# Edge stage of a graph network: block sums in float32r in two parts, and gathered rows in a ring of six quads

## Reference

```python
msg_in = jnp.concatenate([x[src], x[dst], edge_attr], axis=-1)
msgs = jnp.maximum(msg_in @ mW1 + mb1, 0.0) @ mW2 + mb2
agg = jax.ops.segment_sum(msgs, dst, num_segments=num_nodes)
cnt = jax.ops.segment_sum(jnp.ones((dst.shape[0],), x.dtype), dst, num_segments=num_nodes)
...
msg = h[src] + h_edge_attr
agg = jax.ops.segment_sum(msg, dst, num_segments=n)
```

## Time and profile before

| | us |
|---|---|
| median of three timed runs | 4918.04 (4917.9 to 4919.48) |
| span of the profiled execution | 5506.7 |
| PE busy, PEld busy | 4490.6, 3990.8 |
| DVE busy | 3075.2 |
| ACT busy | 1937.4 |
| POOL busy | 2459.1 |
| mean granted TensorE clock | 0.916 of full |

### The profile page before, as it was taken

One profiled execution on the slowest core, in us unless ns is written; L12 is line 12 of the kernel. 1 busy time (PEld: TensorE's weight loads), 2 busy tenths in 40 slices (PEclk: granted clock), 3 DMA queues, 4 the chain that ended last, 5 costly groups with the idle time before them and its releaser, 6 DMA issues. The chain is left out here.

```text
span 5506.7 us, 112775 instructions
## 1 busy us (share of the span) xinstructions
PE 4490.6 (82%) x38465; PEld 3990.8 (72%) x38465; DVE 3075.2 (56%) x7918; ACT 1937.4 (35%) x4103; POOL 2459.1 (45%) x2823
## 2 busy tenths in 40 slices
PE   0499999999666777777777877787778999888887
PEld 0399999999555666666666766676667666788887
DVE  5699999998333333333333333333334444688788
ACT  0556666665211111111111111111112444555666
POOL 5411111110466566566666656666662100465565
PEclk9799999999777888888888888888889999999999
DMA  4344444444444555555555555555557555666665
GB/s 107 130 199 210 210 210 209 201 202 201 145 113 126 156 162 165 155 163 160 164 162 158 164 162 164 159 164 164 165 168 209 182 187 187 204 208 208 221 216 181
DMA packets 571498, 966.86 MB, mean 176 GB/s; under 512 B 101223, under 2 KB 418775, under 8 KB 552519
## 3 DMA queue, kind: packets, MB, share of 16 engines
q1 hardware_dynamic: 407520, 767.32, 39.7%
q0 software_dynamic: 60048, 125.37, 8.8%
q10 hardware_dynamic: 103767, 72.40, 5.3%
HBM read 707.25 MB, written 257.60 MB: 175 GB/s over the span
## 5 line engine op out<-in xcount | busy, mean ns | idle before, releaser
L1022 POOL DMA_INDIRECT BIG<-table,BIG x1715 | 1697.2, 990 | 1166.0 <-DVE BIG L2454 557.6
L2454 DVE TENSOR_TENSOR BIG<-ps,BIG 128x512 f32<-128x512 f32 (+1 forms) x441 | 297.2, 674 | 1308.1 <-issue 905.6
L1822 PE MATMUL ps<-BIG 128*128 128x257 f32 x3430 | 953.3, 421 | 75.8 <-issue 44.5
L1822 PEld LDWEIGHTS ps<-BIG 128*128 128x128 f32 x3430 | 691.8, 213 | 210.3 <-issue 81.7
L1262 ACT ACTIVATE BIG<-BIG 128x512 f32<-128x512 f32 (+1 forms) x441 | 273.5, 620 | 1583.5 <-DVE BIG L2454 1318.4
L1837 PE MATMUL ps<-H_R,EXACT 128*128 128x256 f32 x4802 | 634.4, 288 | 96.6 <-DVE EXACT L2642 65.2
L1552 PE MATMUL ps<-H,ACC 128*128 128x128 f32 x4802 | 689.9, 284 | 0.0
L1837 PEld LDWEIGHTS ps<-H_R,EXACT 128*128 128x128 f32 x4802 | 591.9, 192 | 120.9 <-DVE EXACT L2642 88.0
L1810 PE MATMUL ps<-ACC,BIG 128*128 (+1 forms) x5145 | 525.1, 236 | 149.0 <-issue 131.9
L1552 PEld LDWEIGHTS ps<-H,ACC 128*128 128x128 f32 x4802 | 588.0, 191 | 0.2 <-ACT ACC L1203 0.2
L1810 PEld LDWEIGHTS ps<-ACC,BIG 128*128 128x128 bf16 x5145 | 420.1, 106 | 223.2 <-issue 186.2
(11 more groups left out here) (293 smaller groups left out, 7915.4 us busy)
## 6 DMA issues: line engine op xcount, KB each, us to landing
weight_mat<-ACC SPq DMA_DIRECT2D x49, 3136.0 KB, 9.2
BIG<-in_edge_attr SPq DMA_DIRECT2D x392, 256.0 KB
X<-count_mat SPq DMA_DIRECT2D x98, 800.0 KB, 4.4
count_mat<-BIG SPq DMA_DIRECT2D x49, 1568.0 KB, 12.8
X<-count_mat SPq DMA_DIRECT2D x98, 768.0 KB, 4.3
REL_WT<-weight_mat SPq DMA_DIRECT2D x275, 256.0 KB
BIG<-rel_tab ACTq DMA_DIRECT2D x392, 128.0 KB
BIG<-weight_mat SPq DMA_DIRECT2D x176, 256.0 KB
```

Source lines behind the costliest of these rows:

```text
L1022: pool.indirect_dma_start(G[:, q * QUAD + u, :], None, tables[1], bass.IndirectOffsetOnAxis(ap=STEP_IDX[:, b % 3, r * QUAD + u:r * QUAD + ...
L1822: mm = pe.matmul(PS[4 + par][:, 0:2 * F + 1], D[q * QUAD + u], HE[:, q * QUAD + u, :], start=(r == 0 and u == 0), stop=(r == QB - 1 and u ...
L2454: dve.tensor_tensor(HE[:, steps, 0:F], PS[n % 2][:, 0:size * F].rearrange("p (u f) -> p u f", f=F), G[:, steps, :], ALU.add).then_inc(rows ...
```

## The change

ReLU rows and attributes are each written twice, as a float32r part and as what it leaves (HI and LO_R), and the f32 product of a step becomes two float32r products, 258 and 256 columns wide, into the same sums. The first part of the attributes is a Copy on ACT, its rest a subtraction on DVE; the first part of the ReLU rows is the ReLU itself, now written to HI, its rest max(row, 0) minus HI on DVE. The gathered rows land in GR, a ring of six quads, are summed in place, and a place is free when the rest of the ReLU rows is made (`hidden_lo`). The attributes land in ATTR, a ring of four quads. The one-hots are written as float32r. The sums of a block leave PSUM in two copies, and ACC's space holds the new rings. DVE's order at position n becomes: turned one-hots, one-hots and attributes' rest of n, sum of n-1, weight group sums, ReLU rows' rest of n-1, then the rest as before.

```diff
--- before.py
+++ after.py
...
 QB = len(SIZES)
 QN = BLOCKS * QB
 EQ = 3
-GATHERS = [sum(SIZES[m % QB] for m in range(n % EQ, n + 1, EQ)) for n in range(QN)]
+GQ = 6
+AQ = 4
+GATHERS = [sum(SIZES[m % QB] for m in range(n % GQ, n + 1, GQ)) for n in range(QN)]
 DONE = [(b + 1) * QB for b in range(BLOCKS)]
 BLOCK_DONE = {n: b for b, n in enumerate(DONE)}
...
+        def of_acc(at, n):
+            return ACCf[:, at:at + n], at + n
+
+        HI_AT, LO_AT, DR_AT = 0, EQ * QUAD * HIW, EQ * QUAD * (HIW + 2 * F)
+        HI = nc.alloc_sbuf_tensor_at("HI", [P, EQ * QUAD, HIW], FP32R, offset=big_at + HI_AT * 4)
+        LO_R = nc.alloc_sbuf_tensor_at("LO_R", [P, EQ * QUAD, 2 * F], FP32R, offset=big_at + LO_AT * 4)
+        DR = nc.alloc_sbuf_tensor_at("DR", [P, EQ * QUAD, P], FP32R, offset=big_at + DR_AT * 4)
+        DTB_, at = of_big(DR_AT + EQ * QUAD * P, EQ * QUAD * P // 2)
+        DTB = DTB_.bitcast(BF16).rearrange("p (s f) -> p s f", f=QUAD * P)
+        STEP_, at = of_big(at, 3 * BSTEPS)
+        STEP_IDX = STEP_.bitcast(I32).rearrange("p (k s) -> p k s", s=BSTEPS)
+        assert at <= 7 * 2 * FSRC * P
+        HIDDEN_T, at = of_big(7 * 2 * FSRC * P, P)
+        NEW_B, at = of_big(at, P)
+        assert at <= 9232
+        ATT_, at = of_acc(0, BLOCKS * (F + 1))
+        ATT = ATT_.rearrange("p (b f) -> p b f", f=F + 1)
+        HS_, at = of_acc(-(-at // 16) * 16, 3 * F)
+        HS = [HS_[:, k * F:(k + 1) * F] for k in range(3)]
+        QP_, at = of_acc(at, 2 * PARTS * F // 2)
+        QP = [QP_[:, k * PARTS * F // 2:(k + 1) * PARTS * F // 2].bitcast(BF16) for k in range(2)]
+        ATTR_, at = of_acc(at, AQ * QUAD * F)
+        ATTR = ATTR_.rearrange("p (s f) -> p s f", f=F)
+        GR_, at = of_acc(at, GQ * QUAD * F)
...
             def attr_part(n, first):
-                r, q = n % QB, n % EQ
-                if n >= EQ:
-                    sp.wait_ge(quad_summed, n - EQ + 1)
-                sp.dma_start(HE[:, q * QUAD:q * QUAD + SIZES[r], F:2 * F],
+                r, q = n % QB, n % AQ
+                if n >= AQ:
+                    sp.wait_ge(attr_lo, ATTR_LO0 + n - AQ + 1)
+                sp.dma_start(ATTR[:, q * QUAD:q * QUAD + SIZES[r], :],
                              attr128[bass.ds(first + r * QUAD * P, SIZES[r] * P), :].rearrange("(u p) f -> p u f", p=P)).then_inc(attr_in[q], 16)
 
...
 
             def edge_gathers():
                 for n in range(QN):
-                    b, r, q = n // QB, n % QB, n % EQ
+                    b, r, q = n // QB, n % QB, n % GQ
                     if r == 0:
                         pool.wait_ge(staged, b + 1)
-                    if n >= EQ:
-                        pool.wait_ge(rows_added, n - EQ + 1)
+                    if n >= GQ:
+                        pool.wait_ge(hidden_lo, HIDDEN_LO0 + n - GQ + 1)
                     for u in range(SIZES[r]):
-                        pool.indirect_dma_start(G[:, q * QUAD + u, :], None, tables[1],
-                                                bass.IndirectOffsetOnAxis(ap=STEP_IDX[:, b % 3, r * QUAD + u:r * QUAD + u + 1], axis=0)).then_inc(gathered[q], 16)
+                        pool.indirect_dma_start(GR[:, q * QUAD + u, :], None, tables[1],
+                                                bass.IndirectOffsetOnAxis(ap=STEP_IDX[:, b % 3, r * QUAD + u:r * QUAD + u + 1], axis=0)).then_inc(rows_in[q], 16)
 
             pool.sem_inc(acc_ready, 1)
...
 
+            def attr_rounded(n):
+                r, q, g = n % QB, n % EQ, n % AQ
+                act.wait_ge(attr_in[g], 16 * (n // AQ + 1))
+                if n >= EQ:
+                    act.wait_ge(quad_summed, n - EQ + 1)
+                act.activation(HI[:, q * QUAD:q * QUAD + SIZES[r], F:2 * F], ATTR[:, g * QUAD:g * QUAD + SIZES[r], :], ACT.Copy).then_inc(attr_hi, 1)
+
             def dense_quad(n):
-                r, q = n % QB, n % EQ
+                r, q, g = n % QB, n % EQ, n % GQ
                 act.wait_ge(rows_added, n + 1)
                 if r == 0 and 1 <= n // QB < BLOCKS - 2:
                     stage_block(n // QB + 2)
-                hidden = HE[:, q * QUAD:q * QUAD + SIZES[r], 0:F]
-                act.activation(hidden, hidden, ACT.Relu).then_inc(relu_done, 1)
+                act.activation(HI[:, q * QUAD:q * QUAD + SIZES[r], 0:F], GR[:, g * QUAD:g * QUAD + SIZES[r], :], ACT.Relu).then_inc(relu_done, 1)
                 if n + EQ < QN:
                     load_edges(n + EQ)
 
             def q_part1(b):
-                act.activation(ACCB[:, b, 0:F], T1[:, b, :], ACT.Copy).then_inc(q_high, 1)
+                act.activation(QP[b % 2][:, 0:F], T1[:, b, :], ACT.Copy).then_inc(q_high, 1)
 
             def q_part2(b):
                 act.wait_ge(q_rest, PASSED + b + 1)
-                act.activation(ACCB[:, b, F:2 * F], T1[:, b, :], ACT.Copy).then_inc(q_mid, 1)
+                act.activation(QP[b % 2][:, F:2 * F], T1[:, b, :], ACT.Copy).then_inc(q_mid, 1)
 
             def act_quad(i, q, more):
...
@@ -1421,7 +1458,10 @@
                 act.wait_ge(q_sb, C1 + 1)
                 q_part1(0)
                 q_part2(0)
+                attr_rounded(0)
                 for n in range(POSITIONS):
+                    if n + 1 < QN:
+                        attr_rounded(n + 1)
                     if n < QN:
                         dense_quad(n)
                     if n in PARTS_AT:
...
                     for k in range(PARTS):
-                        pe.matmul(to, DTB[:, q, u * P:(u + 1) * P], ACCB[:, b, k * F:(k + 1) * F], start=(k == 0), stop=False)
+                        pe.matmul(to, DTB[:, q, u * P:(u + 1) * P], QP[par][:, k * F:(k + 1) * F], start=(k == 0), stop=False)
                     mm = pe.matmul(to, A18[:, q, u * P:(u + 1) * P], w18[:, :], start=False, stop=True)
                 mm.then_inc(pre_ps, 1)
 
             def dense_sums(b, r, par):
                 q = r % EQ
-                pe.wait_ge(relu_done, b * QB + (r + 1))
                 pe.wait_ge(onehot_ready, b * QB + (r + 1))
-                pe.wait_ge(attr_in[q], b * (16 * QB // EQ) + 16 * (r // EQ + 1))
+                pe.wait_ge(attr_lo, b * QB + (r + 1 + ATTR_LO0))
+                pe.wait_ge(hidden_lo, b * QB + (r + 1 + HIDDEN_LO0))
                 if r == 0 and (not isinstance(b, int) or b >= 2):
                     pe.wait_ge(block_out, b + (PASSED - 1))
                 for u in range(SIZES[r]):
-                    mm = pe.matmul(PS[4 + par][:, 0:2 * F + 1], D[q * QUAD + u], HE[:, q * QUAD + u, :],
-                                   start=(r == 0 and u == 0), stop=(r == QB - 1 and u == SIZES[r] - 1))
+                    one = DR[:, q * QUAD + u, :]
+                    pe.matmul(PS[4 + par][:, 0:HIW], one, HI[:, q * QUAD + u, :], start=(r == 0 and u == 0), stop=False)
+                    mm = pe.matmul(PS[4 + par][:, 0:2 * F], one, LO_R[:, q * QUAD + u, :], start=False, stop=(r == QB - 1 and u == SIZES[r] - 1))
                 mm.then_inc(quad_summed, 1)
 
...
-                dve.wait_ge(gathered[q], GATHERED0 + 16 * GATHERS[n])
+                r, g = n % QB, n % GQ
+                steps, size = slice(g * QUAD, g * QUAD + SIZES[r]), SIZES[r]
+                dve.wait_ge(rows_in[g], ROWS0[g] + 16 * GATHERS[n])
                 dve.wait_ge(pre_ps, n + 1)
+                dve.tensor_tensor(GR[:, steps, :], PS[n % 2][:, 0:size * F].rearrange("p (u f) -> p u f", f=F), GR[:, steps, :], ALU.add).then_inc(rows_added, 1)
+
+            def dense_attr_rest(n):
+                r, q, g = n % QB, n % EQ, n % AQ
+                steps, own = slice(q * QUAD, q * QUAD + SIZES[r]), slice(g * QUAD, g * QUAD + SIZES[r])
+                dve.wait_ge(attr_hi, ATTR_HI0 + n + 1)
                 if n >= EQ:
                     dve.wait_ge(quad_summed, n - EQ + 1)
-                dve.tensor_tensor(HE[:, steps, 0:F], PS[n % 2][:, 0:size * F].rearrange("p (u f) -> p u f", f=F), G[:, steps, :], ALU.add).then_inc(rows_added, 1)
+                dve.tensor_tensor(LO_R[:, steps, F:2 * F], ATTR[:, own, :], HI[:, steps, F:2 * F], ALU.subtract).then_inc(attr_lo, 1)
+
+            def dense_hidden_rest(n):
+                r, q, g = n % QB, n % EQ, n % GQ
+                steps, own = slice(q * QUAD, q * QUAD + SIZES[r]), slice(g * QUAD, g * QUAD + SIZES[r])
+                dve.wait_ge(relu_done, n + 1)
+                dve.scalar_tensor_tensor(LO_R[:, steps, 0:F], GR[:, own, :], 0.0, HI[:, steps, 0:F], ALU.max, ALU.subtract).then_inc(hidden_lo, 1)
 
             def dense_onehots(n):
                 r, q = n % QB, n % EQ
                 if n >= EQ:
                     dve.wait_ge(quad_summed, n - EQ + 1)
                 step, size = n // QB * BSTEPS + r * QUAD, SIZES[r]
-                dve.tensor_tensor(D_[:, q * QUAD * P:(q * QUAD + size) * P].rearrange("p (u d) -> p u d", d=P),
+                dve.tensor_tensor(DR[:, q * QUAD:q * QUAD + size, :],
                                   iota[:, :].rearrange("p (a d) -> p a d", a=1).broadcast_to([P, size, P]),
```

(21 more changed lines are left out.)

34 lines of the change are left out of this document (17 added, 17 removed).

## The result

The changed kernel takes 5010.8 us (median of four runs, 5007.5 to 5012.4) against 4918.0 us before: a ratio of 1.0191, 95% interval 1.0178 to 1.0203. That is 93 us more; the forecast was 182 us more. The sign and the kind of cause hold (gathers on POOL held up by operations on DVE), the size of that term does not.

What follows compares the result with a forecast made beforehand. The prediction took POOL's gathers to bound the edge stage in timed runs. It added 180 us for gathers delayed by DVE and 0 for all else to 4918, giving 5098, said as 5100 us, range 4700 to 5250.

Steps and rivals of the forecast that it cites:

- What bounds the kernel: Edge stage: POOL's gathers bound it in timed runs, 2183 us, with PE about 10% behind.
- PE: Edge stage: PE at full clock needs 1950 us, about 10% behind POOL.
- Block sums: Block sums on PE: float32r products at 0.125 instead of 0.24 us save 400 us of PE, costed at nothing.
- Ring: Ring of six quads for POOL's gathered rows: taken as 0, ends 0 and 22 us.
- DVE and ACT: Edge stage: 626 us more work on DVE and 270 us on ACT, adding nothing to the time by itself.
- The holds: Edge stage: two new two-input DVE operations delay POOL's gathers, 0.184 us each per quad; +180 us taken.
- The forecast's other bound: POOL's gathers: from the measured mean, 0.13 us per operation and quad, 116 us for two more.
- A: Rival, edge stage: PE's late completions are also there in timed runs; 260 us faster, 4660 us; chance 0.17.
- B: Rival, edge stage: POOL's issue is quicker unprofiled, ring waits remain; 20 to 200 us less, 4800 us; chance 0.15.
- C: Rival, edge stage: delays fall into gaps or new operations do not hold POOL; no change, 4918 us; chance 0.10.
- D: Rival, block sums: float32r sums at the f32 price; PE stays behind POOL, forecast stands; no chance given.

Runs made afterwards that it cites:

- the second profile: The kernel before, unchanged, profiled once more: 4911.1 us, span 4909.0 us.
- the shortened rests: The changed kernel with DVE's two rests cut to one column a step, low halves left out: 4930.7 us, 1.0034 of before.
- the pair of extra operations: The kernel before with two more DVE operations a quad: one-hots with two SBUF inputs, 4981.3 us; sums with one input in PSUM, 4920.0 us.

## Why the prediction came out as it did

**What bounds the kernel: right.** The inferred 2183 us for the edge stage in a timed run is 2201.6 us from the first to the last gather of the undisturbed profile, 1.284 us apart on average. No pause is over 0.32 us. The two are close partly by luck: 42 of the excess us were not in this stage, and the window that the 2183 were taken from reached past the last gather. Fewer gathers bring 385 us, a longer ring nothing.

**PE: too high, without effect.** I put its need at 1950 us, 10% behind POOL. With two gathers fewer the stretch is 1767.5 us from first to last gather, at 97% busy PE: 20% behind. My sum of pieces was not checked against a busy time at full clock, for which no row existed.

**Block sums: right, as to PE's work.** L1863 and L1864 start 0.12 us apart, 0.95 us for a quad's eight against 1.90; I had 0.125. PE's busy time in the stage falls by 184 us, less than the 400, and its granted clock falls from 0.94 to 0.85. Busy time times clock, an estimate of the work at full clock, goes from 1753 to 1429 us, 325 less. By this estimate the clock takes up most of the gap, and some 75 us of it stay unexplained. It costs and brings nothing behind POOL.

**Ring: right**, 0 of a range of 0 to 22 us. **DVE and ACT: right**, 559 and 242 us more busy against 626 and 270, nothing of it on the path by itself. That is so only under POOL's cover: with the cover gone the change costs 118 us more than it wins, a point that the forecast did not have.

**The holds: right in kind, wrong in size.** This is the term of the sum that was mis-sized: "at a random phase one of 0.68 us catches a gather with chance 0.54, for 0.34 us on average: 0.184 us". Measured are 0.095 us (L2507) and 0.099 us (L2501) per operation and quad: 41.8 and 43.5 us over 441. By the table above an operation must start before the gather does and still run 0.13 us into it. That leaves starts in a stretch of 0.68 − 0.13 − 0.03 = some 0.52 us (the 0.03 for the row from 0.05 to 0, where not all are held), and holds from 0 to 0.52 us, 0.26 on average. As an estimate that is 0.52/1.28 × 0.26 = 0.106 us for a quad of four steps and, with 0.56 us operations, 0.06 for the 49 quads of three: 0.10 us on average. The same random phase, with the right window, gives the measured number. Two operations cost 85 us, the one-hots, at their new place, 8 more: 93, by the counts above, against 97.3 us that the gathers' busy time rose by.

The forecast's other bound, by the mean of the earlier trace rows, gave 0.13 us and 116 us for two. It was nearer and still too high: it took a mean of 990 ns from the disturbed execution instead of 980 ns, and put all of the excess down to one operation, which holds 38 of some 42 us. I went to the upper of the two values by an argument of phases where the row that measured the thing itself was the safer choice. The mean gather, expected at 1050 ns or more, came to 1036. The range of 4700 to 5250 us holds the time because it was drawn wide, for the rivals; it says nothing for the term.

Of the rivals, A fell with the second profile. B (POOL's issue is quicker unprofiled) fell with it as well: the profiled execution took 4911.1 us, the timed ones beside it have a median of 4912.9. C (the new operations do not hold POOL) fell with the shortened rests and the pair of extra operations. D (float32r at the f32 price) fell with the 0.12 us.

## What to carry to other kernels

When one engine issues back to back, look at what makes its instructions longer before counting what it waits for: sort them by the work that ran at their start, and subtract busy and idle time separately. On a kernel bound by GpSimd's indirect DMAs, a VectorE operation of 0.68 us with two SBUF inputs cost some 0.10 us on average at a random phase, and nothing with one input in PSUM. A tensor_scalar holds a gather as well while it runs; one operation of 0.68 us written as four of 0.3 still won 34 us, by its shortness as I read it. If a profiled span stands 12% above the timed runs, profile again before reading its waits.

## What the hardware showed that I had not expected

- One profiled execution of the kernel before had PE completions many us late and a span of 5506.7 us; the next had 4909.0. Why is open.
- The hold needs the operation to have begun before the gather. Where both began together (1399.77) the gather kept 0.95 us and the operation took 0.04 us more.
- Tensor_scalar operations with one SBUF tensor input held gathers too (638 of 696 by the count above), and the gather ended the same 0.83 us after them. BATCH_NORM_STATS2, with one SBUF input, did not (1 of 82), nor did work with an input in PSUM (3 of 2427).
- A gather already held by one operation was not held again by the next one behind it (1401.03), so two such operations in a row catch less than twice.
- The idle time in front of 1715 gathers was 625.7 to 627.0 us in nine of the ten traces with 1715 gathers, all but the first profile of before, whatever DVE, ACT and PE did.
- PE's granted clock in the stage fell from 0.94 to 0.85 with the change. Behind POOL no time shows for it. With POOL out of the way it is 0.93 against 1.00, and likely part of the 118 us.
